# Sorted rows of a top-4 mixture of experts: lists in memory that hold the token's row itself, read by plain transfers

## The reference

```python
x = adapter(x, cond)                      # down, relu, up, residual; weights per sequence
h = rmsnorm(x) ; q, k, v = h @ qkv_w + qkv_b   # 16 heads, 4 KV heads, 64 wide, rotary, sinks
x2 = x + attention(q, k, v) @ proj_w + proj_b
h2 = rmsnorm(x2)                          # 4096 tokens x 256
topv, topi = top_k(h2 @ gate_w + gate_b, 4)
gw = softmax(topv)
for e in range(32):                       # wu: 256 x 512, wd: 256 x 256
    u, g = split(h2 @ wu[e])
    y2 += combine[:, e] * ((silu(g) * u) @ wd[e])
out = x_in + x2 + y2
```

## Time and profile before

| | us |
|---|---|
| median of 3 runs | 1194.93 (1192.1 to 1195.15) |
| the profiled execution | 1196.22 |
| its span in the trace | 1194.3, at a mean granted clock of 0.93 |

### The profile page before, as it was taken

The page is one execution under the profiler, slowest core; times in us unless marked ns, Lnnn a source line. Parts: engine busy times, 40 slices in busy tenths (PEclk is TensorE's granted clock), DMA queues, the critical chain, the costliest instruction groups (busy, mean ns, idle before and its releaser), DMA issues.

```text
span 1194.3 us, 18647 instructions
## 1 busy us (share of the span) xinstructions
PE 990.4 (83%) x6190; PEld 798.9 (67%) x6190; DVE 766.7 (64%) x1712; ACT 455.6 (38%) x1128; POOL 716.1 (60%) x676
## 2 busy tenths in 40 slices
PE   3789799998999999998833878888978888988985
PEld 2557576776777676776622767777767777877774
DVE  3868487786867777784661555656656556556577
ACT  1133243434243353424511444444435344444441
POOL 3426346858586776767584656666666666666650
PEclk9779899999999999998965999998999999998998
DMA  5328877565657666556566756465655556552399
GB/s 175 86 65 275 311 256 202 186 185 191 190 171 240 205 199 198 188 170 215 196 211 230 240 186 243 155 237 183 230 194 195 189 186 215 187 189 74 86 349 337
DMA packets 110951, 239.46 MB, mean 200 GB/s; under 512 B 19311, under 2 KB 48388, under 8 KB 110119
## 3 DMA queue, kind: packets, MB, share of 16 engines
q1 hardware_dynamic: 84042, 192.03, 49.1%
q0 software_dynamic: 19760, 40.32, 10.9%
q10 hardware_dynamic: 7056, 5.91, 1.6%
HBM read 140.66 MB, written 90.32 MB: 193 GB/s over the span
## 4 chain that ended last, share of the span: by engine, by line
PE 57%; DVE 19%; issue 8%; POOL 4%; DMA 4%; another core or an unknown queue 4%; ACT 3%; SPq 0%; POOLq 0%; DVEq 0%; ACTq 0%
PE gbank L858 9%; PE gbank L990 8%; PE scores L990 6%; PE gbank L1009 4%; DVE ring L1349 4%; PE gbank L783 4%; PE scores L819 4%; PE scores L1009 3%; POOL lists L660 3%; PE gbank L999 2%; PE gbank L761 2%; DVE in_part L1580 2%; DVE mid L1588 2%; PE scores L999 1%
## 5 line engine op out<-in xcount | busy, mean ns | idle before, releaser
L705 POOL DMA_INDIRECT pick_rows<-rows_out,pair_row x158 | 163.5, 1035 | 141.3 <-ACT rows_out L1218 98.6
L698 POOL DMA_INDIRECT rows_in<-x_rows,token_row x158 | 154.1, 975 | 54.5 <-issue 43.6
L667 POOL TENSOR_TENSOR ring<-ring 128x512 fp32r<-128x512 f32 x96 | 121.1, 1280 | 72.5 <-ACT ring L1159 71.1
L660 POOL DMA_INDIRECT lists<-entry,slot_i x128 | 125.3, 979 | 38.8 <-issue 34.2
L858 PE MATMUL gbank<-w_o,ring 128*128 128x256 f32 x512 | 128.1, 407 | 14.8 <-DVE ring L1332 12.1
L990 PE MATMUL gbank<-ring,in_part 128*128 x480 | 139.4, 428 | 0.0
L990 PE MATMUL scores<-ring,in_part 128*128 x486 | 138.0, 421 | 0.0
L783 PE MATMUL gbank<-h_t,w_qk 128*128 128x512 f32 x480 | 120.8, 405 | 7.3 <-DVE h_t L1336 4.2
L858 PEld LDWEIGHTS gbank<-w_o,ring 128*128 128x128 f32 x512 | 103.2, 205 | 35.2 <-ACT ring L1129 16.3
L1349 DVE SCALAR_TENSOR_TENSOR ring<-gbank,b_qk,rope 128x512 f32<-128x512 f32 x160 | 108.5, 743 | 5.3 <-PE gbank L783 5.1
L783 PEld LDWEIGHTS gbank<-h_t,w_qk 128*128 128x128 f32 x480 | 89.7, 192 | 29.9 <-issue 5.8
(11 more groups left out here) (189 smaller groups left out, 1917.8 us busy)
## 6 DMA issues: line engine op xcount, KB each, us to landing
w_parts<-ring SPq DMA_DIRECT2D x192, 256.0 KB
ring<-w_parts SPq DMA_DIRECT2D x32, 1536.0 KB
ring<-in_W_up SPq DMA_DIRECT2D x64, 256.0 KB
picks<-pick_rows SPq DMA_DIRECT2D x8, 2048.0 KB, 27.8
lists<-in_fill_slots SPq DMA_DIRECT2D x36, 256.0 KB, 4.9
ring<-in_W_down SPq DMA_DIRECT2D x32, 256.0 KB
q_r<-rot SPq DMA_DIRECT2D x16, 512.0 KB, 6.1
q_r<-ring SPq DMA_DIRECT2D x16, 512.0 KB
```

Of the source, the lines that this page charges most:

```text
L660: e.indirect_dma_start(out=lists, out_offset=bass.IndirectOffsetOnAxis(ap=slot_i[pb][:, k:k + 1], axis=0), in_=entry[pb][:, k, :], in_offs ...
L667: e.tensor_tensor(lower, lower.bitcast(F32), upper.bitcast(F32), ALU.subtract).then_inc(s_lower, 1)
L698: e.indirect_dma_start(out=rows_in[i % NG][:, :], out_offset=None, in_=x2_rows, in_offset=bass.IndirectOffsetOnAxis(ap=begun[:, i, 3:4].bi ...
L705: e.indirect_dma_start(out=pick_rows, out_offset=bass.IndirectOffsetOnAxis(ap=begun_row[:, i:i + 1] if i < AHEAD else pair_row[:, i:i + 1] ...
```

## The change

The lists in memory now hold, for each pair, the token's row of x2 itself (256 floats) and behind it the entry: ROW = 272 floats, 1,088 bytes. The put scatters such rows. A tile of sorted rows is then one stretch of memory of 139 KB, and is read by one plain transfer, issued by ACT, at an address which the plan gives. Gate, norm factor and pair number are read out of the loaded rows.

- Removed: `fill_lists` (37 transfers of SP in block 1), the 161 gathers of POOL, its two list gathers, `turn_lists`, the `begun` load, `columns` and `slots` of DVE, and one DVE operation per routing group (token number).
- Added on ACT in part 1: `pack` (x2's row copied four times into `put_rows`, a 128x1024 copy) and `tag` (the 16 entries' columns), one each per tile of tokens, with places in the written orders. `put_rows` has two buffers, and four more for the last eight tiles, in space of `q_r` and `rot`.
- Fills: three of 139 KB in `load_late` (behind the three first tiles, and the spare tile), and 32, one at the end of each expert's list, issued by SP in the transition, behind the ring loads of experts 1 to 3 and ahead of the waits that tell PE of them, at addresses that DVE makes (`fill_at`), read into registers eight at a time.
- Added in part 2: ACT's `load_rows`, six tiles ahead, ten buffers; `load_row_at`, one read of eight addresses every eight tiles; DVE's copy of one column to `pair_i` in each `turn_in`. PE makes one more plan row (`list_row`). POOL only scatters.
- The stores of `x2_rows` and the load of `resid` stay.

```diff
-NW, NU, NPAY, NG, NY, NC = 5, 3, 3, 8, 6, 4
+NW, NU, NPAY, NG, NY, NC = 5, 3, 3, 10, 6, 4
+ROWS_AHEAD = NG - 4
+NPUT, NLATE = 2, 4
...
         turn_prob softmax_a sums attend root apply split route_turn split project route_turn split
-        softmax_a turn_prob route_turn route_turn attend route_pick split turn_prob split project split
-        attend softmax_a split turn_prob split project split down attend split softmax_a up split split
-        project
+        softmax_a turn_prob route_turn route_turn attend route_pick split pack pack turn_prob split project split
+        attend softmax_a tag tag split turn_prob split project split down attend split pack tag softmax_a
+        up split split project pack tag
...
+        route_turn softmax_a split route_turn attend route_pick split pack pack pack pack project split
+        root tag tag tag tag turn_prob attend softmax_a split route_turn route_turn split project
+        turn_prob root attend split route_pick pack pack split split tag tag project split route_turn
+        root pack route_turn pack route_pick tag route_pick tag
...
-    lists = nc.dram_tensor("lists", (E * LIST + P, LINE), F32, kind="Internal").ap()
+    lists = nc.dram_tensor("lists", (E * LIST + P, ROW), F32, kind="Internal").ap()
...
-        def fill_lists(c):
-            at = slice(c * FILL_ROWS, min((c + 1) * FILL_ROWS, E * LIST + P))
-            e.dma_start(lists[at, :], d["fill_slots"][0:at.stop - at.start, :]).then_inc(s_fill, 16)
+            for at in [n * LIST + P for n in range(1, AHEAD)] + [E * LIST]:
+                e.dma_start(lists[at:at + P, :], d["fill_rows"]).then_inc(s_fill, 16)
...
         for n in range(1, RING):
             load_expert(n)
+        w.wait_ge(s_fill, FIRST_FILL)
+        w.wait_ge(s_fill_at, 1)
+        for k in range(E // BATCH):
+            _, at = nc.values_load_multi_w_load_instructions(
+                fill_at[0:1, k * BATCH:(k + 1) * BATCH], engines=[mybir.EngineType.SP], min_val=0,
+                max_val=(E * LIST - P) * ROW, skip_runtime_bounds_check_because="an expert has at most NTOK rows")
+            for n in range(BATCH):
+                e.dma_start(lists_flat[bass.ds(at[n], P * ROW)].rearrange("(p w) -> p w", w=ROW), d["fill_rows"]).then_inc(
+                    s_fill, 16)
         for n in range(1, RING):
             say_ready(n)
...
         def route_put(t):
+            w.wait_ge(s_fill, FIRST_FILL)
             w.wait_ge(s_slot_i, r + 1)
-            w.wait_ge(s_fill, FILL)
-            for k in range(s * TOPK, (s + 1) * TOPK):
+            w.wait_ge(s_packed, t + 1)
+            w.wait_ge(s_tagged, t + 1)
+            for k in range(TOPK):
                 e.indirect_dma_start(
-                    in_=entry[pb][:, k, :], in_offset=None).then_inc(s_entry[pb], 16)
+                    in_=put_rows[put_at[t]][:, k, :], in_offset=None).then_inc(s_listed[put_at[t]], 16)
...
-        for i in range(AHEAD, NG - 1):
-            gather(i)
-        for i in range(NET + 4):
-            if i + NG - 1 < NET:
-                gather(i + NG - 1)
-            if i >= 4:
-                scatter(i - 4)
+        for i in range(NET):
+            scatter(i)
...
+        def pack(t):
+            w.wait_ge(s_x2, t + 1)
+            if put_at[t] in put_at[:t]:
+                w.wait_ge(*listed(max(u for u in range(t) if put_at[u] == put_at[t])))
...
+            e.activation(put_rows[put_at[t]][:, :, 0:D], x2[m % 2][:, s, :].unsqueeze(1).to_broadcast([P, TOPK, D]),
+                         ACT.Copy).then_inc(s_packed, 1)
+        def tag(t):
+            w.wait_ge(s_slot_i, r + 1)
+            e.activation(put_rows[put_at[t]][:, :, D:D + 4], entry[r % NPAY][:, s * TOPK:(s + 1) * TOPK, :],
+                         ACT.Copy).then_inc(s_tagged, 1)
...
+        def load_rows(i):
+            if i >= NG:
+                w.wait_ge(s_rows_out, i - NG + 1)
+            if i < AHEAD:
+                rows = lists[i * LIST:i * LIST + P, :]
+            else:
+                rows = lists_flat[bass.ds(row_at[i // BATCH][i % BATCH], P * ROW)].rearrange("(p w) -> p w", w=ROW)
+            e.dma_start(rows_in[i % NG][:, :], rows).then_inc(s_rows_in[i % NG], 16)
+        for t in sorted(max(u for u in range(NT) if put_at[u] == b) for b in range(NPUT + NLATE)):
+            w.wait_ge(*listed(t))
+        w.wait_ge(s_fill, FILL)
+        for i in range(AHEAD):
+            load_rows(i)
+        w.wait_ge(s_plan_list, 1)
+        load_row_at(0)
+        for i in range(AHEAD, ROWS_AHEAD):
+            load_rows(i)
...
             if i >= 3:
                 expert_down(i - 3)
+            if (i + ROWS_AHEAD) % BATCH == 0 and i + ROWS_AHEAD < NET:
+                load_row_at((i + ROWS_AHEAD) // BATCH)
+            if i + ROWS_AHEAD < NET:
+                load_rows(i + ROWS_AHEAD)
...
         def turn_in(i):
             w.wait_ge(s_in_upper, i + 1)
+            e.tensor_copy(pair_i[:, i:i + 1], rows_in[i % NG][:, D:D + 1])
```

More of the change, by code:

```diff
@@ L38 @@
 LINE = 16
-FILL_ROWS = 32 * P
-FILLS = -(-(E * LIST + P) // FILL_ROWS)
+ROW = D + LINE
 PAIRS = NTOK * TOPK
@@ L364, in program @@
     all_out = sb("all_out", [1, 1], I32)
-    rows_in = [sb(f"rows_in{i}", [P, D]) for i in range(NG)]
+    rows_in = [sb(f"rows_in{i}", [P, ROW]) for i in range(NG)]
     in_parts = [[sb(f"in_part{i}{h}", [P, KC, P], F32R) for h in range(2)] for i in range(IN_BUFS)]
@@ L619, in gpsimd_program @@
             e.memset(entry[i][:, :, :], 0.0)
+        for i in range(NPUT):
+            e.memset(put_rows[i][:, :, D:ROW], 0.0)
         e.memset(eps[:, :], EPS).then_inc(s_memset, 1)
@@ L1186, in scalar_program @@
                 route_pick(k)
+            elif name == "pack":
+                pack(k)
+            elif name == "tag":
+                tag(k)
             elif name == "split":
@@ L1210, in expert_up @@
             e.activation(silu[i % 2][:, :], front[i % FRONTS][:, DFF:2 * DFF], ACT.Silu,
-                         scale=begun[:, i, 2:3] if i < AHEAD else norms[:, i:i + 1]).then_inc(s_silu, 1)
+                         scale=rows_in[i % NG][:, D + 2:D + 3]).then_inc(s_silu, 1)
         def expert_down(i):
@@ L1218, in expert_down, with load_row_at @@
             e.activation(rows_out[i % NY][:, :], back[i % BACKS][:, D:2 * D], ACT.Copy,
-                         scale=begun[:, i, 1:2] if i < AHEAD else gates[:, i:i + 1]).then_inc(s_rows_out, 1)
-        for r in range(GROUPS - NPAY, GROUPS):
-            w.wait_ge(s_entry[r % NPAY], entries_of(r))
-        e.dma_start(begun[:, :, :], lists[0:AHEAD * LIST, :].rearrange("(n r) w -> r n w", n=AHEAD)[0:P, :, 0:4]).then_inc(
-            s_begun, 16)
+                         scale=rows_in[i % NG][:, D + 1:D + 2]).then_inc(s_rows_out, 1)
+        row_at = {}
+        def load_row_at(k):
+            _, row_at[k] = nc.values_load_multi_w_load_instructions(
+                plan_list[0:1, k * BATCH:(k + 1) * BATCH], engines=[mybir.EngineType.Activation], min_val=0,
+                max_val=E * LIST * ROW, skip_runtime_bounds_check_because="the plan holds places of list tiles")
+        def load_rows(i):
[3 more added lines that the diff above has]
+                rows = lists[i * LIST:i * LIST + P, :]
+            else:
+                rows = lists_flat[bass.ds(row_at[i // BATCH][i % BATCH], P * ROW)].rearrange("(p w) -> p w", w=ROW)
[5 more added lines that the diff above has]
+            load_rows(i)
+        w.wait_ge(s_plan_list, 1)
+        load_row_at(0)
+        for i in range(AHEAD, ROWS_AHEAD):
+            load_rows(i)
         turn_in(0)
         turn_in(1)
-        w.wait_ge(s_begun, 16)
         for i in range(NET + 3):
@@ L1450, in route_list @@
             if r >= NPAY:
-                w.wait_ge(s_entry[pb], entries_of(r - NPAY))
+                m0, lo0, hi0 = ROOTS[r - NPAY]
+                for t in range(TPM * m0 + lo0, TPM * m0 + hi0):
+                    w.wait_ge(*listed(t))
             w.wait_ge(s_memset, ONES)
```

162 lines of the change are left out of this document (53 added, 109 removed).

## The result

The kernel after takes 1129.34 us (median of 4 runs, 1127.93 to 1132.2) beside 1195.04 for the kernel before (4 runs, 1192.1 to 1199.23): ratio 0.9457, 95% interval 0.9434 to 0.948. Forecast were 1117 us and 1095 to 1175. But that is the result of one chip. On a second one, with the same two programs, the kernel before takes 1103.94 us and the kernel after 1118.03: ratio 1.0136, interval 1.0106 to 1.0165, so the change makes it 1.4% slower there. On the four chips of the experiments the kernel before took 1103.9 to 1111.4 us (two medians of 13 runs, two single runs), never 1195.

What follows compares the result with a forecast made beforehand. PE, busiest in the expert stage, was thought held up by some 95 us of gaps from POOL's transfer trains. -85 - 4 + 6 + 0.5 + 5 = -77.5 us gave 1117 us, range 1095 to 1175.

Steps and rivals of the forecast that it cites:

- gathers gone: Expert stage: with one scatter per tile left on POOL, PE's gaps of some 95 us nearly vanish, -85 us.
- theory A: Expert stage: long trains of POOL's software transfers delay other engines' signals; gathers put back should give 1190 to 1225 us.
- the first rival: Expert stage: gaps not caused by POOL, so none come back; +7.5, 1202 us, slower; chance 0.09.
- the stretch 828 to 851: Expert stage, kernel before: cited as POOL having pauses (busy 15.75 of 23.00 us) and PE no gap.
- Fills gone from block 1: Block 1 of attention: list fills removed, -4 us, at least 2.5 and at most 7.1.
- The chain's one wait: Block 1: 7.13 us of issue ahead of the scores, rotated queries behind fills; gave the upper bound 7.1.
- Packs and tags: Attention on ACT: each block's fourth pack adds 1.0 us in six blocks, +6; last block +0.5 (0 to 2).
- Transition: Between routing and experts: 32 fills added, begun load and list gathers removed; +5 us, -3.5 to +9.
- Rows late: Expert stage: row loads behind weight bursts land after their lead; 17 us at 7.6 us landing; over 1199, chance 0.04.
- The lead of 7.0 us: Expert stage: a row load is issued some 7.0 us before PE turns its rows, so barely covered, cost 0.

Runs made afterwards that it cites:

- the five runs with gathers: Kernel after with a gather per tile that nothing reads put back on POOL: 1 KB rows 1117.05, 1127.49, 1134.15 us; 64-byte rows 1113.01, 1115.40 us.
- The spread fills of section 4: Kernel before with its 37 list fills spread over the blocks instead of all in block 1: 1100.98 us against 1104.22, ratio 0.9971.
- short packs: Kernel after with each pack on ACT shortened to 128x16 elements, puts unchanged: 1112.57 us.
- the nine traces: Traces that have the kernel after's attention stage unchanged; their blocks 2 to 6 take 349.8 to 360.0 us, 355 in the mean.
- short puts: Kernel after with full packs, but each put scattering and each row load reading only the entry's 64 bytes: 1105.49 us.
- the two issuers of fills: Kernel after with 16 of the 32 late fills issued on ACT instead of SP: 1115.81 us, beside 1118.03 for the kernel after; ratio to before 1.0119.

## Why the prediction was right, and where it was not

**The gaps.** The step "gathers gone", -85, measured -92.2 on the chip whose trace it was read from: the stretch fell to PE's own pace. That POOL with single transfers leaves no gaps was read rightly from the end of the stage. The reading behind it, that trains of software transfers delay the signals between the other engines, is half of the truth. What stands: on the first chip the signal was late. PE's up product begun at 693.41 was done at 695.05, ACT was free from 696.91, and its silu began at 699.81. Timelines of PE, ACT and DVE, kernel before:

```profile
693.41 1.64 PE L990 MATMUL gbank<-ring,in_part 128*128 x6
```

```profile
696.28 0.63 ACT L1204 ACTIVATE in_part<-scores,norm_w 128x128 fp32r<-128x128 f32 x2 [1.67 <-PE gbank L964]
699.81 0.47 ACT L1210 ACTIVATE silu<-gbank,norms 128x256 f32<-128x256 f32 x1 [2.90 <-remote]
```

```profile
700.32 0.48 DVE L1588 SCALAR_TENSOR_TENSOR mid<-gbank,norms,silu 128x256 f32<-128x256 f32 x1 [2.77 <-issue]
```

The prediction speaks of signals between the other engines. The trace shows more narrowly that the late ones were PE's. DVE took ACT's signal here 0.04 us after silu's end. The trace also holds the times at which semaphores were raised. Each raise was set against the last end before it of an instruction that raises this semaphore, so that a lateness is at least what is given. In the expert stage of the kernel before: of 561 raises by PE 53% came over 0.3 us late, the latest 5.1 us; of 453 by DVE and 350 by ACT none came over 0.02 us late. PE's work itself seems to have been done in time, though the ends of matmuls are modelled here: the raise that was due at 697.6, behind six matmuls of 1.6 us, came at 701.41, only 0.07 us after the one for the transposes ahead of them. In the kernel after on the same chip 0.5% of PE's raises in that stage are over 0.3 us late, the latest by 0.5 us. In its attention stage, where POOL still issues its puts in fours, 4% are, by up to 3.3 us. In the expert stage of the kernel before on the second chip, and of the five runs with gathers on three further ones, none of PE's is over 0.02 us late. So for the first chip theory A gains support: with POOL's second transfer the late signals went, and with them the gaps. The change altered the row loads too, so it is not a clean test.

Two readings of the prediction are weaker than it has them. The silu of 699.81 began while POOL was still in its last gather (699.03 to 700.00), so a signal doesn't wait for the train's end. And the stretch 828 to 851 is no case of POOL with pauses throughout: from 839.76 it issued twelve transfers without one, and PE's gap followed at 853.9. PE's records hold 20 gaps of over 2 us between 658 and 1154, not 38.

What fell: that a train is enough for it. On four other chips longer trains than any in the first trace delay nothing. What the first chip has besides stays open, and so does whether it belongs to that chip for good or to its state in that hour. Theory A could not be tried on it, since no later run was placed there, and neither could the first rival, gaps of another cause. That its single scatters make no gaps is the one thing that its own pair of traces shows.

**Fills gone from block 1**, -4 forecast, -10.1 and -8.6 measured; the upper bound was 7.1. The chain's one wait was taken for the whole cost. The row that had it was the window of the block: a DMA share of 0.88 in this block only, PE idle for 10 of its 71 us, and a clock of 0.93. Without fills PE is idle for 2.9 us, the clock is 1.00 and PE busy 58.1 instead of 61.05 us for the same instructions. The spread fills of section 4 show the same, 62.1 us at a clock of 1.00, with nothing else of the change.

**Packs and tags**, +6 in six repeats of the written order, of which five are blocks 2 to 6 and the sixth lies in the last window: +5 there, +16.4 and +15.5 measured, and +1.5 in the last window with its own +0.5, +8.9 and +7.2 measured. This is the term that was mis-sized. The mechanism that it names, packs that lengthen PE's wait at the projection, is in the traces and not larger than forecast: with short packs PE's two waits are 2.4 to 4.6 us shorter than in the nine traces. What it left out is the puts. Their seventeen times as many bytes were costed on POOL, where indeed a put still takes 0.96 to 0.98 us, and not in the queues, through which the weights, the moved queries and the stores of that stage go: the DMA share rises from 0.64 to 0.68, PE waits some 6 us more for the queries, and the short puts give 10 us back. Part of the loss is PE's clock: it is busy 321.93 instead of 312.96 us in blocks 2 to 6 and 99.52 instead of 91.77 in the last block, with the same instructions, at a granted clock of 0.96 for 0.98 and 0.84 for 0.91. One projection of 16 products, kernel before, then after, where the granted clock was 1.00 and 0.68:

```profile
262.87 3.62 PE L858 MATMUL gbank<-w_o,ring 128*128 128x256 f32 x16
```

```profile
256.95 5.30 PE L832 MATMUL gbank<-w_o,ring 128*128 128x256 f32 x16
```

**Transition**, +5 forecast (-3.5 to 9), +12.5 and +6.7 measured, the first outside that range. The first turn came at 675.35 and not at 651 to 658: 15.4 us of that is the late start of the ring loads (630.40 for 615.05), which is the attention terms again, net of block 1; the fills took 29.4 us of issuing with their address reads where 20 to 26 were forecast, on the second chip 24.1. Timeline of SP and of PE, first chip, kernel after:

```profile
630.40 9.02 SPq L553 DMA_DIRECT2D ring<-w_parts  x4
641.61 29.43 SPq L579 DMA_DIRECT2D lists<-in_fill_rows  x32
```

```profile
675.35 1.22 PE L932 MATMUL scores<-ident,rows_in 128*128 128x128 f32 x4 [36.80 <-DMA rows_in<-lists]
```

**Rows late.** The rival did not come about: PE waits 0.8 us in all for them. The lead of 7.0 us was met closely: from a load's issue to the turn of its rows it is 7.5 us in the median. The two row loads on the chain of waits took 7.69 and 7.89 us, and each was issued 0.7 to 1.7 us behind one of the 28 weight loads (788.93 and 869.63). List of waits of PE, 690 to 1064 us, and chain of waits, kernel after:

```profile
PE scores L932 <- DMA rows_in<-lists: 0.8, 1, 0.8
```

```profile
790.65 7.69 DMA rows_in<-lists
...
870.36 7.89 DMA rows_in<-lists
```

By the Trainium skill, DMA: Bandwidth & Descriptors, Issuing engines are not separate DMA queues, all issuers' transfers share 16 engines; the two issuers of fills (DMA share 1.02 either way) and the 8.0 us of waits for rows beside gathers that nothing reads agree with it.

**The sum** was -77.5 and came out at -67.2: 7 us better in the gaps, 6 in block 1, 3 in the tail, and 26 worse in attention and transition (11.4, 7.4 and 7.5). The errors are as large as any term but the gaps, and partly cancel. So 1129.3 us lie within the range, 12 above the forecast. That it holds is also luck: it was compared on the very chip whose trace it was read from. On the second chip the forecast is wrong, and by the step that was its largest: there are no gaps to give back, the outcome of the first rival, whose +7.5 us stand against 14.1 measured. The kernel after did not run on the other three, but the kernel before's 1104 to 1111 us leave no room for such gaps there.

## What to carry to other kernels

A wait that the profile calls remote, and that no program order explains, may belong to the chip that made the trace: run the kernel before on a second chip before a change is built on removing it, and look whose signal came late and by how much. Cost a wider transfer in the queues of the whole stage, not only on the engine that issues it. When a block stands out from its neighbours in DMA share, its difference in length from them does not bound the price of what is peculiar to it: here the difference was 2.5 us and the price 8 to 10, and the block's own idle time and granted clock showed it.

## What the hardware showed that was not expected

The same program took 1195 us on one chip and 1104 to 1111 us on four others. Where it was traced again, the attention stage was alike to 3.3 us (524.65 and 521.40 from block 1 to the ring loads) and the expert stage took 470.34 against 380.62. On the slow one a release was taken 4.8 us after the product was done (699.81 for 695.05), in a train in which POOL issued gather and scatter in turn. Only PE's signals were late there, half of them, while those of ACT and DVE in the same trains came within 0.02 us; with scatters alone on the same chip PE's were at most 0.5 us late.
